# Closing stage of an attention and mixture-of-experts kernel: who adds the two copies of the sums, and in which order VectorE works

## The reference

```python
x = x + layernorm(attention(layernorm(x)))      # 16 query heads, 4 key/value groups, causal
x = x + layernorm(moe(layernorm(x)))            # 64 experts, top 6, capacity 64, and a shared expert
```

## Time and profile before

| | |
|---|---|
| median of 3 runs | 1496.03 us (1494.36 to 1497.07) |
| profiled execution, its own time | 1492.12 us |
| its span in the trace | 1490.0 us |
| mean granted TensorE clock in it | 0.957 |
| busy: PE, PE weight load, DVE, ACT, POOL | 1357.7, 1200.7, 1104.1, 837.3, 791.5 us |
| closing stage, from the issue of the first load to the end of the span | 1431.83 to 1490.0 us |

### The profile page before, as it was taken

The page is one execution under the profiler, slowest core; times in us unless marked ns, Lnnn a source line. Parts: engine busy times, 40 slices in busy tenths (PEclk is TensorE's granted clock), DMA queues, the critical chain, the costliest instruction groups (busy, mean ns, idle before and its releaser), DMA issues. The chain is left out here.

```text
span 1490.0 us, 27249 instructions
## 1 busy us (share of the span) xinstructions
PE 1357.7 (91%) x9155; PEld 1200.7 (81%) x9155; DVE 1104.1 (74%) x3547; ACT 837.3 (56%) x2283; POOL 791.5 (53%) x1030
## 2 busy tenths in 40 slices
PE   3899999999999999999999999999999995499920
PEld 3799999999999999999999999999999994344410
DVE  4867686889688977897789778977887686444447
ACT  4666665666566666666566656666666661144423
POOL 2555564546454655565546554655555541355555
PEclk9899999999999999999999999999999996799965
DMA  8100000100010001000100010001000057299973
GB/s 279 56 1 1 15 15 9 33 22 15 2 40 22 15 1 40 22 15 1 40 22 15 2 40 22 15 1 40 23 2 15 26 143 248 62 305 307 278 238 124
DMA packets 49610, 95.97 MB, mean 64 GB/s; under 512 B 4193, under 2 KB 36418, under 8 KB 49474
## 3 DMA queue, kind: packets, MB, share of 16 engines
q1 hardware_dynamic: 43330, 84.80, 17.0%
q0 software_dynamic: 6144, 9.44, 3.1%
HBM read 67.74 MB, written 26.48 MB: 63 GB/s over the span
## 5 line engine op out<-in xcount | busy, mean ns | idle before, releaser
L1486 POOL TENSOR_TENSOR prob<-prob,rinv 128x512 f32<-128x512 f32 (+3 forms) x512 | 366.6, 726 | 350.5 <-DVE rinv L1159 347.6
L870 ACT ACTIVATE prob<-prob,negmax 128x512 f32<-128x512 f32 (+3 forms) x512 | 282.9, 555 | 9.1 <-DVE negmax L1152 8.3
L1473 POOL TENSOR_TENSOR q_l<-q_sum,q_h 128x128 fp32r<-128x128 f32 (+1 forms) x256 | 183.5, 738 | 27.0 <-ACT q_h L850 24.9
L532 PE MATMUL bank_o<-pt_h,v_h 128*128 128x128 f32 (+3 forms) x512 | 179.5, 351 | 0.0
L532 PE MATMUL bank_o<-pt_h,v_l 128*128 128x128 f32 (+3 forms) x512 | 165.2, 323 | 0.0
L532 PE MATMUL bank_o<-pt_l,v_h 128*128 128x128 f32 (+3 forms) x512 | 164.8, 322 | 0.0
L532 PE MATMUL bank_y<-wo_h,o_h 128*128 128x256 f32 x512 | 143.9, 281 | 2.6 <-DVE o_l L1170 2.4
L532 PE MATMUL bank_y<-wo_h,o_l 128*128 128x256 f32 x512 | 143.5, 280 | 0.0
L532 PE MATMUL bank_y<-wo_l,o_h 128*128 128x256 f32 x512 | 143.2, 280 | 0.0
L879 ACT ACTIVATE pt_h<-bank_t 128x512 fp32r<-128x512 f32 (+3 forms) x210 | 90.0, 429 | 84.4 <-PE bank_o L532 66.7
L886 ACT ACTIVATE o_h<-bank_o,bkv_s 128x512 fp32r<-128x512 f32 x128 | 88.0, 688 | 81.2 <-PE bank_o L532 80.8
(11 more groups left out here) (379 smaller groups left out, 4254.8 us busy)
## 6 DMA issues: line engine op xcount, KB each, us to landing
w_gu<-in_w_in SPq DMA_DIRECT2D x32, 704.0 KB
w_dn<-in_w_out SPq DMA_DIRECT2D x32, 352.0 KB
xio<-in_x SPq DMA_DIRECT2D x16, 512.0 KB, 3.9
token_table<-rows SPq DMA_DIRECT2D x8, 640.0 KB, 3.7
ffn_sums<-keys SPq DMA_DIRECT2D x4, 1024.0 KB
x_rows<-xio SPq DMA_DIRECT2D x8, 512.0 KB, 2.9
ffn_sums<-ytr SPq DMA_DIRECT2D x16, 256.0 KB, 2.1
fx<-x_rows SPq DMA_DIRECT2D x8, 512.0 KB, 9.2
```

Of the source, the lines that this page charges most:

```text
L532: return pe.matmul(o, l, r, start=start, stop=stop, skip_group_check=True)
L870: act.activation(p_, p_, ACT.Exp, bias=negmax[:, r, i:i + 1], scale=-1.0, accum_out=rsum[:, r, i:i + 1]).then_inc(exp_made, 1)
L1473: pool.tensor_tensor(l_[:, cols], q_sum[:, cols], plain(h_)[:, cols], ALU.subtract).then_inc(pos_low, 1)
L1486: pool.tensor_tensor(p_, p_, rinv[:, r, i:i + 1].to_broadcast([P, (i + 1) * P]), ALU.mult).then_inc(prob_made, 1)
```

## The change

VectorE makes the whole sum (four rows, 128x1024), and GpSimdE none of it. The helper `variance` is taken apart into `statistics(b)` and `aggregates(b)`. VectorE's queue gets a new order: sum(b), statistics(b), residual(b-2), bias(b-1), aggregates(b). So VectorE makes sum and statistics of a batch before it turns to the bias of the batch before, and the residual comes one round later than it did. The wait between statistics and aggregates stays, with the other two steps between them. No tile, DMA, activation or power instruction is changed.

```diff
             def add_sums(b):
                 dve.wait_ge(dma_f[b], 32)
-                dve.tensor_tensor(fa[b][:, TT - 1:TT, :], fa[b][:, TT - 1:TT, :], fb[b][:, TT - 1:TT, :], ALU.add
-                                  ).then_inc(sum_dve, 1)
-
-            def variances(b):
-                dve.wait_ge(sum_pool, b + 1)
+                dve.tensor_tensor(fa[b][:], fa[b][:], fb[b][:], ALU.add).then_inc(sum_dve, 1)
+
+            def statistics(b):
                 dve.wait_ge(sum_dve, b + 1)
-                variance([fa[b][:, k, :] for k in range(TT)], fstat[b % 2], fmv[b % 2], fnw[b])
+                for k in range(TT):
+                    last = dve.bn_stats(fstat[b % 2][:, k, :], fa[b][:, k, :])
+                last.then_inc(stats_made, 1)
+
+            def aggregates(b):
+                for k in range(TT):
+                    last = dve.bn_aggr(fmv[b % 2][:, k, :], fstat[b % 2][:, k, :])
+                last.then_inc(var_made, 1)
...
             for b in range(NB):
                 add_sums(b)
+                statistics(b)
+                if b > 1:
+                    residual_out(b - 2)
                 if b:
                     bias(b - 1)
-                variances(b)
-                if b:
-                    residual_out(b - 1)
+                dve.wait_ge(stats_made, b + 1)
+                aggregates(b)
             bias(LAST)
+            residual_out(LAST - 1)
             residual_out(LAST, 2)
...
-            def add_sums(b):
-                pool.wait_ge(dma_f[b], 32)
-                pool.tensor_tensor(fa[b][:, 0:TT - 1, :], fa[b][:, 0:TT - 1, :], fb[b][:, 0:TT - 1, :], ALU.add
-                                   ).then_inc(sum_pool, 1)
-
             for b in range(NB):
-                add_sums(b)
                 inverse_root(fmv[b % 2], fnw[b], TT)
```

More of the change, by code:

```diff
@@ L244, in build @@
             sem(f"e_{n}") for n in ("same_made", "target_made", "second_made", "same_in"))
-        sum_pool, sum_dve, bias_made, final_normed, final_made = (
-            sem(n) for n in ("sum_pool", "sum_dve", "bias_made", "final_normed", "final_made"))
+        sum_dve, stats_made, bias_made, final_normed, final_made = (
+            sem(n) for n in ("sum_dve", "stats_made", "bias_made", "final_normed", "final_made"))
         vec_step, pool_step = sem("vec_step"), sem("pool_step")
```

## The result

| | before | after |
|---|---|---|
| median of 5 runs | 1496.61 us (1494.36 to 1501.29) | 1482.58 us (1478.78 to 1484.9) |
| ratio, 95% interval | | 0.9887 (0.9859 to 0.9915) |
| profiled execution, its span | 1492.12, 1490.0 us | 1482.58, 1480.8 us |

The account below looks back on a forecast made before the run. TensorE bounds the whole kernel, a GpSimdE-VectorE ring the closing stage; rounds of 4.24 against 6.06 us plus the ends save 14.2, taken as 14: 1496.03 - 14 = 1482.0 us, range 1479.5 to 1484.5 (1479 to 1487.5 with A and most of B).

Parts of the forecast that it names:

- The ring over two engines: Closing stage: GpSimdE's sum of b+1 queues behind its power of b, which needs sum b; 6.06 us a round.
- Parts 1 to 3: Closing-stage round: GpSimdE's sum (1.79 us) goes, VectorE's whole sum takes 1.23, VectorE's new round is 4.24 against 6.06.
- Part 4: GpSimdE's epsilon, held by the sum, ends at about 1.25 us after the aggregates; the power takes 1.05, ends at 2.38.
- The cover of 0.14 us at the residual's start: Time from the end of GpSimdE's power to the start of VectorE's residual; forecast 0.16 us.
- the cover at the bias: Time from the end of GpSimdE's power until VectorE's bias is due; forecast 1.3 us.
- Part 5: Loads: sum 1 waits 0.2 us for its load of 6.8 us; then a batch lands every 2.6 us, hidden.
- Part 6: ScalarE: 2.07 us a round, hidden except at the end, where activations 7 follow those of 6 at once.
- A: Closing stage: residual gets in front of the power; round 5.2 us, gain 9 us, time 1487; chance 0.07.
- B: Closing stage: epsilon starts ahead of the next sum, which waits; round 4.5 to 5.5 us, time 1483 to 1488.5; chance 0.05.
- C: Closing stage held by transfers: last stores queue up or loads arrive later; 1483.3 to 1484.6 us; chance 0.07.
- D: GpSimdE's late answer makes the bias wait every round; from 6.5 us on 3 us slower, 1499; chance 0.02.
- E: No change: the ring isn't what bounds the closing stage, and the time is made up elsewhere; chance 0.03.

Follow-up runs that it names:

- the changed kernel once more: The changed kernel run again, unaltered, on the same chip (its second trace): median 1481.11 us, ratio 0.9862, closing stage 43.0 us.

## Why the prediction was right

**What bounded the stage.** The ring over two engines, GpSimdE's sum behind its own power, was the bound: with the order alone the ring stays, and with it the time (6.22 us a round); with the sum alone it goes, and so do 11.2 us.

**Parts 1 to 3, the round.** Forecast 4.24, measured 4.03 us, which over five rounds is 1.0 us. The sum took 1.22 us from start to start instead of 1.26, the statistics 1.32 instead of 1.36, the residual 1.13 instead of 1.15, the aggregates 0.29 instead of 0.30. The one term that was mis-sized is the bias: 0.07 us from its start to that of the aggregates, not 0.17. I had taken its full duration, though the rows already showed that a following VectorE instruction starts up to 0.08 us before the end of the one ahead.

**Part 4, GpSimdE's answer.** Epsilon was held by the sum to 1.11 us (forecast: about 1.2), and the power ran beside the statistics in 1.04. The cover of 0.14 us at the residual's start was of no account: a power that has started 0.17 us earlier is past any hold. Only the cover at the bias counts. It is 1.27 us; one more power fitted in it in the middle rounds, and two more did not. My sentence that the residual might catch the power's tail had no ground, as the run with one more power showed.

**Part 5, the loads.** The step that was off. Sum 1 started 4.76 us after sum 0, not 3.33, because its load landed after 8.2 us instead of 6.8. This differs from run to run: the changed kernel once more had 3.55, others lay between 3.20 and 4.85. Why it varies isn't shown. It took 1.4 us back and nearly cancelled the gain on the rounds. From batch 2 on no load was waited for, as forecast, though for batch 2 the margin was only 0.5 us: its load landed at 1448.6, and the sum started at 1449.11.

**Part 6 and the end.** Activations 7 followed those of 6 without a gap, as forecast. The last residual started 3.58 us before the end of the span; 3.48 was forecast, 3.18 it was before. All terms together: 14.2 forecast, + 1.0 for the rounds, - 1.4 for the load of batch 1, and + 0.1 for the rest, gives 13.9. That the sum came out so close is in part luck, since two errors of opposite sign nearly cancel. In the changed kernel's second trace the second of them is almost gone, and the stage is 15.2 us shorter. The median of 1482.58 us against the forecast 1482.0 owes more to luck still: it rests on the part before the closing stage as well, which varies by several us from run to run.

**The rivals.** A, the residual in front of the power, did not happen, but its price was right: 1.0 us a round when an edit brought it about. B did not happen: epsilon started 0.17 us after the sum in each round. C: the transfers set only the first wait; with the residual cut the round fell by all that VectorE was spared. D, the slower one: an answer of 2.3 us (from 1453.23 to 1455.55) against a cover of 3.6. E is excluded by the traces. The profile's difference of 9.2 us would have looked like a forecast of 14 missed by a third, were it not for the 4.7 us by which the untouched part ended later.

## What to carry to other kernels

When no engine is full in a stage and the chain of waits alternates between two engines, look for the instruction that stands in an engine's queue behind an answer it doesn't need; taking that one away is the gain, and a new order alone is worth nothing while the ring stands. Then count the cover of the remote answer to the place where it is consumed, by inserting known work in front of it: here 1.0 us more was free in the middle rounds, though it cost 1.1 us at the two ends of the stage, and 2.0 us more cost 1.0 us in every round. When one ring is broken, look for the next: with the sum alone moved it was the one over VectorE and ScalarE, and the new order was what opened it. Compare a change in a short stage by the length of that stage; the untouched rest of this kernel ended up to 14.7 us apart between traces.

## What the runs showed of the hardware

- The hold between GpSimdE and VectorE depends on who starts first, and a power of 128x4 escapes it with a lead of 0.05 us. A power that started 0.05 us after a two-tile VectorE instruction took 2.08 us and ended 0.90 us behind it; started 0.25 us into it, 1.86 us and 0.89 behind it; started 0.80 us into it, 1.27 us and 0.86 behind it. Started 0.05, 0.09 or 0.17 us ahead of it, it took 1.05, 1.05 and 1.01 us, and 1.04 with no VectorE instruction beside it. The VectorE instruction was never longer for it (1.21 to 1.23 us).
- Statistics (one tile as input) hold nothing: the power beside them took 1.04 us in every middle round.
- A DMA that adds 512 KB from DRAM onto SBUF took 8.5 to 14.9 us, 9.7 in the median, from issue to landing beside plain loads and later stores. The first three landed 3.8 and 3.7 us apart, the later ones 2.5 to 3.9, where a pair of plain loads, twice the bytes, landed every 2.5 us, the last one after 3.1 (kernel before, loads of batches 1 to 7).
